# Storing the query rows' mean and deviation in the hop loops and loading them in the rounds

## The reference, cut to what matters

```python
x = x + xattn(_layernorm(x), ctx_1024, ctx_1024, ...)
x = x + ffn(_layernorm(x), ...)

def _layernorm(x, axis=-1, eps=1e-05):
    m = jnp.mean(x, axis=axis, keepdims=True)
    v = jnp.var(x, axis=axis, keepdims=True)
    return (x - m) / jnp.sqrt(v + eps)

# in xattn: q = the normed rows, k = v = ctx
pe = rpe[hops].reshape(Sq, Sq, NH, DH)
k_hop = einsum('bhvc,vmhc->bhvm', qh, pe)      # first use of q
qk = einsum('bhsd,bhtd->bhst', qh, kh / sqrt(DH))   # second use of q
C = (qk + k_hop) * D
```

## Time and profile before

| | |
|---|---|
| median of 3 runs | 4463.74 us (4459.74 to 4472.94) |
| the profiled execution, its own time | 4464.32 us |
| its span in the trace | 4462.6 us |
| hop loops | to about 1841 us |
| rounds | from about 1841 us to the end |
| busy share of the span: PE, DVE, POOL, ACT | 83%, 60%, 49%, 43% |
| mean granted clock of PE | 0.947 of full |

### The profile page before, as it was taken

How to read it: one execution, slowest core, us unless ns; L and a number is a source line. 1 busy time by engine, 2 the same in 40 slices (tenths; PEclk the granted TensorE clock), 3 DMA queues, 4 the chain that set the end, 5 groups by cost and what they waited for, 6 DMA issues and landing times.

```text
span 4462.6 us, 82557 instructions
## 1 busy us (share of the span) xinstructions
PE 3690.6 (83%) x21556; PEld 2143.2 (48%) x21556; DVE 2695.9 (60%) x5561; ACT 1925.9 (43%) x4449; POOL 2188.5 (49%) x2567
## 2 busy tenths in 40 slices
PE   6777878878777877688889888888888888988897
PEld 4555544444444444345445444444444444544443
DVE  4545444444344444377777777777676776777774
ACT  3544444444344434354444444444444444444442
POOL 4567667777677777233333333333333333333332
PEclk9999989999999999799999999999999999999999
DMA  7889989999899999554344344444444434444341
GB/s 219 271 263 304 301 275 313 314 312 313 269 311 316 312 312 313 205 175 143 129 161 151 140 141 134 161 144 137 152 135 157 143 127 162 138 156 135 130 154 47
DMA packets 400329, 912.17 MB, mean 204 GB/s; under 512 B 54234, under 2 KB 152538, under 8 KB 391924
## 3 DMA queue, kind: packets, MB, share of 16 engines
q1 hardware_dynamic: 297716, 574.59, 37.5%
q0 software_dynamic: 102400, 335.63, 23.9%
HBM read 708.17 MB, written 201.85 MB: 204 GB/s over the span
## 4 chain that ended last, share of the span: by engine, by line
PE 31%; DVE 17%; issue 7%; ACT 2%; DVEq 1%; DMA 1%; ACTq 0%; SPq 0%; POOL 0%
PE psum L1344 7%; PE psum L1280 5%; PE psum L1288 5%; PE psum L1225 4%; PE psum L1304 3%; PE psum L1258 3%; DVE arena L1011 2%; PE psum L1346 2%; DVE arena L1019 1%; PE psum L1357 1%; DVE arena L1087 1%; DVE arena L991 1%; DVE arena L1082 1%; DVE arena L998 1%; DVE arena L1021 1%
## 5 line engine op out<-in xcount | busy, mean ns | idle before, releaser
L634 POOL DMA_INDIRECT arena<-in_L_xattn_rpe_dram,arena x1280 | 1220.0, 953 | 512.1 <-issue 305.7
L1200 PE MATMUL psum<-arena 128*128 128x128 f32 x5120 | 743.2, 287 | 350.2 <-DMA arena<-in_L_xattn_rpe_dram,arena 169.0
L1200 PEld LDWEIGHTS psum<-arena 128*128 128x128 f32 x5120 | 564.8, 145 | 632.7 <-DVE arena L471 241.3
L471 DVE COPY arena<-psum 128x512 f32<-128x512 f32 x640 | 442.6, 692 | 399.3 <-PE psum L1200 395.9
L471 ACT COPY arena<-psum 128x512 f32<-128x512 f32 x640 | 376.2, 588 | 644.2 <-PE psum L1200 643.8
L1211 PE MATMUL psum<-arena 128*64 128x128 f32 (+3 forms) x4096 | 649.3, 449 | 2.9 <-DVE arena L471 2.2
L654 POOL TENSOR_SCALAR_AFFINE_SELECT arena<-arena 128x256 f32<-128x256 f32 x256 | 113.4, 443 | 1033.2 <-ACT arena L779 1029.7
L479 DVE COPY arena<-psum 128x128 f32<-128x128 f32 (+3 forms) x512 | 251.3, 491 | 536.6 <-PE psum L1211 530.3
L1225 PE MATMUL psum<-arena 128*128 128x128 f32 x2176 | 346.6, 294 | 241.9 <-ACT arena L756 118.5
L779 ACT ACTIVATE arena<-arena 128x512 f32<-128x512 f32 (+3 forms) x1024 | 503.7, 557 | 54.3 <-issue 51.2
L1011 DVE TENSOR_TENSOR arena<-psum,arena 128x1024 f32<-128x1024 f32 (+1 forms) x384 | 400.6, 1043 | 183.9 <-PE psum L1288 159.0
(11 more groups left out here) (100 smaller groups left out, 4427.6 us busy)
## 6 DMA issues: line engine op xcount, KB each, us to landing
hop_products<-arena SPq DMA_DIRECT2D x64, 1024.0 KB, 6.2
arena<-in_x_dram SPq DMA_DIRECT2D x256, 256.0 KB, 4.0
arena<-gate_rows SPq DMA_DIRECT2D x128, 512.0 KB, 3.8
arena<-hop_products SPq DMA_DIRECT2D x128, 512.0 KB, 5.6
hop_products<-arena SPq DMA_DIRECT2D x64, 768.0 KB, 5.4
arena<-hop_products SPq DMA_DIRECT2D x128, 384.0 KB, 4.4
arena<-in_x_dram SPq DMA_DIRECT2D x512, 64.0 KB
hop_products<-arena SPq DMA_DIRECT2D x64, 512.0 KB, 4.7
```

The lines of the kernel that those rows point to most:

```text
L471: copy(rowsT[v % 2][:, :, o[2] * P:(o[2] + 1) * P], bank(1 + n % 2).rearrange("p (k m) -> p k m", k=KT)).then_inc(stage.sem, stage.step(o))
L634: nc.gpsimd.indirect_dma_start(out=rows[v][:, t, :], out_offset=None, in_=rpe[:, :], in_offset=bass.IndirectOffsetOnAxis(ap=here[:, t, v:v ...
L1200: last = nc.tensor.transpose(bank(1 + n % 2)[:, q * P:(q + 1) * P], rows[v][:, o[2], q * P:(q + 1) * P], ident)
```

## The change

- Hop loops: the statistics tile `x_stats` becomes two, one for each parity. After the norm of a group, SP stores mean and 1/deviation of its 128 rows, 8 bytes each, to a new DRAM tensor `query_stats`, ahead of the loads of `x` for the group two later. DVE waits for the store of two groups before, ahead of `bn_aggr`.
- Rounds: SP loads the 512 pairs of a batch (four per partition, 8 bytes each) by one DMA ahead of the four of `xq`. The norm reads them there and waits for this load. The statistics of the query tiles on DVE and their Ln and Exp on ACT are gone.

```diff
-        x_stats = place(8)
+        x_stats = [place(8) for _ in range(2)]
...
-        xq_stats = [place(16) for _ in range(2)]
+        xq_stats = place(ST * 2).rearrange("p (t n) -> p t n", t=ST)
...
+        stats_dram = nc.dram_tensor("query_stats", (S, B, 2), F32).ap()
...
-        X_STATS = [0, 2, 3, 4]
...
+        stats_store = stats_dram.rearrange("(g v) b n -> g (v b) n", v=VG)
+        stats_load = stats_dram.rearrange("(t p) b n -> b p t n", p=P)
...
                     g = k * 2 + par
+                    gg = g + SEG_GROUPS * s
+                    sp.wait_ge(dve_q.sem, dve_q.done(gg, "norm"))
+                    sp.dma_start(stats_store[gg, :, :], x_stats[par][:, 6:8]).then_inc(stats_stored[par], 16)
                     if not last:
-                        gg = g + SEG_GROUPS * s
-                        sp.wait_ge(dve_q.sem, dve_q.done(gg, "norm"))
                         load_group(par, gg + 2)
...
                 sp.wait_ge(dve_p.sem, dve_p.done(r.b, ("norm", ST - 1), 1))
+                sp.dma_start(xq_stats, stats_load[r.b, :, :, :]).then_inc(stats_loaded, 16)
...
-                    for t in at_step(X_STATS, s):
-                        if rp:
-                            act.wait_ge(dve_p.sem, dve_p.done(rp.b, ("mean", t)))
-                            st = xq_stats[t % 2]
-                            rstd(act_p, rp.b, ("ln", t), ("rstd", t), st[:, 7:8], st[:, 7:8])
...
                 dve.wait_ge(dve_q.sem, dve_q.done(g, "stats"))
+                dve.wait_ge(stats_stored[par], half * 16 + 16)
                 stand_alone(dve, "dve")
...
-                def stats_query(t):
-                    st = xq_stats[t % 2]
+                def norm_query(t):
+                    if t == 0:
+                        dve.wait_ge(stats_loaded, rp.b * 16 + 16)
                     dve.wait_ge(xq_loaded[t], rp.b * 16 + 16)
-                    nc.vector.bn_stats(st[:, 0:6], xq[t]).then_inc(dve_p.sem, dve_p.step(("stats", t)))
-                    dve.wait_ge(dve_p.sem, dve_p.done(rp.b, ("stats", t)))
-                    stand_alone(dve, "dve")
-                    nc.vector.bn_aggr(st[:, 6:8], st[:, 0:6]).then_inc(dve_p.sem, dve_p.step(("mean", t)))
-
-                def norm_query(t):
-                    st = xq_stats[t % 2]
-                    dve.wait_ge(act_p.sem, act_p.done(rp.b, ("rstd", t)))
                     dve.wait_ge(pe_p.sem, pe_p.done(rp.b, ("x", (t - 1) % ST), 1 if t < 1 else 0))
-                    nc.vector.tensor_scalar(xq_norm, xq[t], st[:, 6:7], st[:, 7:8], ALU.subtract,
+                    nc.vector.tensor_scalar(xq_norm, xq[t], xq_stats[:, t, 0:1], xq_stats[:, t, 1:2], ALU.subtract,
                                             ALU.mult).then_inc(dve_p.sem, dve_p.step(("norm", t)))
```

More of the change, by code:

```diff
@@ L218, in build @@
         setup_evac = sem("setup_evac")
+        stats_stored = [sem(f"stats_stored{i}") for i in range(2)]
+        stats_loaded = sem("stats_loaded")
         x_group_loaded = [sem(f"x_group_loaded{i}") for i in range(2)]
@@ L284, in build @@
             dve_p_steps += [("norm", t) for t in at_step(X_TURN, s)]
-            for t in at_step(X_STATS, s):
-                dve_p_steps += [("stats", t), ("mean", t)]
             for t in at_step(CENTER, s):
@@ L305, in build @@
                 act_p_steps.append("stats")
-            for t in at_step(X_STATS, s):
-                act_p_steps += [("ln", t), ("rstd", t)]
             pe_p_steps += [("x", t) for t in at_step(X_TURN, s)]
@@ L420, in hops_over @@
                 engine.wait_ge(hop_stored[i], 32 * (GROUPS // 2 + 1))
+            for i in range(2):
+                engine.wait_ge(stats_stored[i], 16 * (GROUPS // 2 + 1))
             engine.wait_ge(dve_q.sem, dve_q.done(GROUPS - 1, "norm"))
@@ L487, in _ @@
                 sp.sem_inc(out_stored[i], 32)
+                sp.sem_inc(stats_stored[i], 16)
             sp.dma_start(hops_raw.bitcast(I32).rearrange("p (t m) -> p t m", t=ST),
@@ L713, in queries, with stats @@
             def queries(par, g):
-                stats(g)
+                stats(par, g)
                 turned(par, g)
-            def stats(g):
+            def stats(par, g):
                 act.wait_ge(dve_q.sem, dve_q.done(g, "mean"))
-                rstd(act_q, g, "ln", "rstd", x_stats[:, 7:8], x_stats[:, 7:8])
+                rstd(act_q, g, "ln", "rstd", x_stats[par][:, 7:8], x_stats[par][:, 7:8])
             def turned(par, g):
@@ L739, in hop_body @@
                         if o == ("prod", 1) and not (last and par):
-                            stats(ahead)
+                            stats(1 - par, ahead)
                         if o == ("prod", VG - 2) and not (last and par):
@@ L908, in query_stats @@
                 dve.wait_ge(x_group_loaded[par], half * 64 + 64)
-                nc.vector.bn_stats(x_stats[:, 0:6], x_group[par]).then_inc(dve_q.sem, dve_q.step("stats"))
+                nc.vector.bn_stats(x_stats[par][:, 0:6], x_group[par]).then_inc(dve_q.sem, dve_q.step("stats"))
                 dve.wait_ge(dve_q.sem, dve_q.done(g, "stats"))
+                dve.wait_ge(stats_stored[par], half * 16 + 16)
                 stand_alone(dve, "dve")
-                nc.vector.bn_aggr(x_stats[:, 6:8], x_stats[:, 0:6]).then_inc(dve_q.sem, dve_q.step("mean"))
+                nc.vector.bn_aggr(x_stats[par][:, 6:8], x_stats[par][:, 0:6]).then_inc(dve_q.sem, dve_q.step("mean"))
             def query_norm(par, g):
@@ L916, in query_norm @@
                 dve.wait_ge(pe_q.sem, pe_q.done(g, "turn", 1))
-                nc.vector.tensor_scalar(x_norm, x_group[par], x_stats[:, 6:7], x_stats[:, 7:8], ALU.subtract,
+                nc.vector.tensor_scalar(x_norm, x_group[par], x_stats[par][:, 6:7], x_stats[par][:, 7:8], ALU.subtract,
                                         ALU.mult).then_inc(dve_q.sem, dve_q.step("norm"))
@@ L1118, in run @@
                         pair_sums(ra, SUMS.index(s))
-                    for t in at_step(X_STATS, s):
-                        if rp:
-                            stats_query(t)
                     for t in at_step(CENTER, s):
```

## The result

The change takes **4555.73 us** (median of 4 runs, 4544.55 to 4560.69) against 4463.36 for the kernel before on the same chip (4 runs). The ratio is 1.0194, with a 95% interval of 1.0173 to 1.0216. The forecast was 4420 us with a range up to 4455; the kernel is 92 us slower. The profiled execution took 4555.6 us of its own, with a span of 4553.9 us.

A forecast was written before the change was run, and what follows sets the result against it. DMA was taken to bound the hop loops, and in the rounds PE's wait behind DVE's queue ahead of the turn. The terms -31 - 14 - 3 + 2 + 2 = -44 took 4464.3 to 4420 us, range 4387 to 4455.

The forecast's parts named there:

- The stores: Hop loops, 128 stores of 128 8-byte runs: priced at 16 to 81 ns per run, +2 us, ends 0 and 83.
- the rival on the slower side: SP's DMA queue, hop loops: stores cost more than the rounds gain, 81 ns a run, 83 us, 4501 us in all; chance 0.06.
- Statistics of tile 0: Rounds, DVE ahead of PE's turn in step 1: removing them gains 1.0 us per round over 31 rounds, -31 us.
- The time is given back: Rival, rounds: POOL's holds catch the early DVE, or PE stays longer at half clock; 4465 us, partly 4455 to 4465; chance 0.15.
- PE's clock: Rounds, behind PE's wait ahead of the turn: a shorter wait loses less to half clock, 0.45 us per round, -14 us.
- First round: First round, where its statistics are on the chain three times: -3 us, between 0 and -4.5.
- DVE in the hop loops: One more DVE wait per group between L909 and L912, 0.05 us each, on the path in segment 0 only: +2 us.
- SP: SP's issuing: a fifth DMA per group finds room in the hop loops, and the rounds' extra load is hidden: 0.
- the loads of the pairs: Rounds, SP's load ahead of `xq`: hidden, since the norm reads over 43 us later: 0.
- Statistics of tiles 1 to 3: Rounds, steps 2, 3, 4, with ACT's Ln and Exp: covered by PE's unbroken work, so removing them gains 0.
- the list of signs: Right: PE's wait ahead of the turn about 3 us, L1115 then L1011 at once, rounds' clock 0.95, hop end within 5 us of 1841.

The follow-up runs named there:

- apart: The kernel before plus a scratch store per group of 128 runs of 8 bytes, target rows 512 bytes apart, no DVE wait: 4464.97 us.
- pitch32: The kernel before plus a scratch store per group of 128 runs of 8 bytes, target rows 32 bytes apart, no DVE wait: 4472.73 us.
- before_both: The kernel before, statistics still computed in the rounds, with ACT's square ahead of step 0's keys and keys ahead of the router's Exp: 4386.2 us, ratio 0.9812.
- wide stores: The change with each pair stored and loaded as a 128-byte row, 30 columns of zeros behind it: 4460.61 us, ratio 0.9979 against the kernel before.

## Why the prediction was wrong

**"The stores": +2 us, ends 0 and 83.** This is the step that failed most: about 100 us, outside its own ends. It priced the packet and asked how much time its own transfer takes. The single packets' records show that this price was even too high: the 8-byte packets took 9 ns each, against 16 and 81 in the two ends. What costs is what stands beside and behind them: with rows 8 bytes apart other packets are stalled, and the gathers, which nobody had touched, land 2.1 us later. That the rival on the slower side, at 0.06, came near is luck in the size: it had the place (SP's queue in the hop loops) and nearly the size (83 us), but its mechanism, 81 ns per run whatever the neighbours, is refuted by `apart` and `pitch32`. The Trainium skill (DMA: Bandwidth & Descriptors, Specifications) was cited there for read-modify-write under 512 bytes. The runs disagree with that as a price: writes of 8 (apart), 32, 64 and 128 bytes were all free here. The Trainium skill (DMA: Bandwidth & Descriptors, How a descriptor splits into AXI transactions) gives 32 bytes as the beat of a transfer; rows that far apart are free here and rows 16 bytes apart aren't, though no run shows what the hardware does inside.

**"Statistics of tile 0": 1.0 us per round, -31.** This failed too: 0.05 us to the first sum in the rounds with the 4.17 us wait, and nothing from L1110 to the turn in the others. In the first kind the step asked what DVE would run into late (POOL's hold of L1038) and not what it would run into next: L1011 needs PE's scores and L1019 needs ACT's square, and both came just in time before. POOL's hold was no larger there: L1041 and L1046 took 0.40 and 0.93 us before, their successors 1.04 and 0.19. In the second kind POOL was the agent after all, though at other instructions than the step had named (L1115 and L1082). "The time is given back", at 0.15, was the right rival: its agent is right in half of the rounds and missing for the other half. Once the keys no longer stood behind the router, loading was worth 34 us. That is near 31 by luck: 16 of it is idle time and 20 is clock, and the forecast had 31 and 14 for the two.

**"PE's clock": -14.** Nothing, since the wait did not shorten. The 1.7 us for a shortened wait was misread as well: rows 7 show a mean clock of 0.64 over 3.4 us there, not half clock throughout, which loses 1.2. Nor does the length of the wait settle the clock: half clock stands behind 4.09 us, 0.64 behind 2.27 and 0.66 behind 1.96 (ahead of 2328.2, `before_both`), but full clock behind the change's 2.05, where PE had been below full clock just before, and behind 1.50 and 1.09.

**"First round": -3** was not measured by itself.

**"DVE in the hop loops": +2,** and **"SP"** and the loads of the pairs, 0: right within what can be told. DVE's wait costs 0.1 us a group, twice the 0.05 taken, and with wide stores the hop loops end where they did (1819.6 against 1818.0). No wait of DVE in the rounds ends with the load of the pairs. **"Statistics of tiles 1 to 3": 0.** Nothing speaks against it: all of DVE's 100 us less work in the rounds is worth 9 us. They were not tried by themselves.

**Against the list of signs:** the hop loops were to end within 5 us of 1841 (their last gather came 99.7 late, with PE waiting for gathered rows, the sign named for "wrong"), PE's idle time ahead of the turn was to fall to about 3 us (it stayed at 3.7 to 4.3), and L1115 was to be followed at once by L1011 (0.57 us of waiting lie between them in one kind of round; in the other it is so, and gains nothing).

## What to carry to other kernels

When a small result is stored next to heavy DMA traffic, lay the rows at least 32 bytes apart or make the runs that long; look at the landing times of the other transfers and not at the small packet's own time. When work is taken off an engine, read in the timeline at what moment each operand of its next two or three instructions becomes ready: an operand that is ready just as the engine comes (0.08 us here) says that another engine is close behind and will set the pace. Look as well at what the earlier small instructions will then stand beside: 0.14 us became 0.90 here behind a POOL operation. And test a removal together with the order that would let it pay, since here it was worth 9 us alone and 34 behind another order.

## What the runs showed of the hardware

- Stores to DRAM of 128 rows that lie 8 or 16 bytes apart stall other transfers of the core: 16384 runs of 8 bytes, four to each 32 bytes, cost 143 us; 16384 of 16 bytes, two to each 32 bytes, about 31; one run per 32 bytes (8 or 32 bytes wide) nothing that the time shows. The same number of 8-byte reads from rows 2048 bytes apart cost nothing.
- The stalled time isn't in the packets that cause it (9 ns each) but in others: the share of busy DMA engines rose from 0.86 to 0.90 while they moved 211 instead of 268 GB/s, and 420 packets instead of 5 took more than 1 us.
- A DVE operation on one column took 0.90 us and ended with a POOL operation that had started 0.20 us ahead of it; started 0.02 us ahead of the POOL operation it took 0.14.
- Half clock can follow a wait of PE of about 2 us: the mean was 0.66 in the 4.7 us behind 1.96 us, and 1.00 behind 1.50.
